# A graph-attention kernel's first-layer node update: bias products on TensorE replaced by adds on VectorE and GpSimd

## The reference, cut to what matters

```python
# layer 0, per node, after the attention sums
out = msgs.reshape(N, H * D) @ Wo + bo
x = out + node_features
mu, var = mean(x), var(x)
layer0 = (x - mu) / sqrt(var + 1e-05) * gamma + beta
x1 = _layernorm(node_features + layer0)
# layer 1, per node
xp = x1 @ W                          # 256 columns; the kernel stores them with the layer's bias less one added
a_src, a_dst = xp . att_src, xp . att_dst   # 4 + 4 columns
```

## Time and profile before

| | us |
|---|---|
| Median of 3 runs | 4633.29 (4626.58 to 4635.58) |
| The profiled execution | 4628.61 |
| Its span, first to last instruction | 4627.2 |
| PE / DVE / ACT / POOL busy in the span | 3929.3 / 3415.2 / 2795.2 / 3143.2 |
| 654 to 2460 us (layer 0's edges at full pace): PE / DVE busy of 1806 | 1710.0 / 1417.4 |

### The profile page before, as it was taken

One profiled execution on the slowest core, in us unless ns is written; L12 is line 12 of the kernel. 1 busy time (PEld: TensorE's weight loads), 2 busy tenths in 40 slices (PEclk: granted clock), 3 DMA queues, 4 the chain that ended last, 5 costly groups with the idle time before them and its releaser, 6 DMA issues. The chain is left out here.

```text
span 4627.2 us, 149696 instructions
## 1 busy us (share of the span) xinstructions
PE 3929.3 (85%) x42462; PEld 2568.6 (56%) x42462; DVE 3415.2 (74%) x11602; ACT 2795.2 (60%) x7985; POOL 3143.2 (68%) x3229
## 2 busy tenths in 40 slices
PE   6988999999999999999996778778877877777874
PEld 4655555555555555555554556555555555555553
DVE  3235788777777778777775578888778778787777
ACT  2324555555555555555553677777777777777775
POOL 1217777777777777777772777777777777777773
PEclk9998999999999999999997677777778777787777
DMA  6878888888888888888884777777777777777774
GB/s 207 282 236 246 259 259 259 257 259 259 259 255 260 258 260 258 257 258 261 259 256 120 187 206 206 207 204 205 207 207 205 205 204 205 205 208 209 203 206 131
DMA packets 820558, 1052.06 MB, mean 227 GB/s; under 512 B 458633, under 2 KB 632338, under 8 KB 820464
## 3 DMA queue, kind: packets, MB, share of 16 engines
q0 software_dynamic: 225072, 726.83, 53.9%
q1 hardware_dynamic: 594078, 323.35, 27.0%
q10 hardware_dynamic: 1314, 0.99, 0.1%
HBM read 915.79 MB, written 133.39 MB: 227 GB/s over the span
## 5 line engine op out<-in xcount | busy, mean ns | idle before, releaser
L1286 POOL DMA_INDIRECT plain_rows<-xp,plain_index x1563 | 1559.8, 998 | 554.9 <-issue 440.8
L765 POOL DMA_INDIRECT typed_rows<-kv,typed_index x1563 | 1511.2, 967 | 626.2 <-issue 414.3
L1391 PE MATMUL plain_p_o<-plain_rows,plain_weight_t 128*64 128x130 f32 (+1 forms) x8336 | 856.5, 348 | 44.0 <-DVE plain_weight_t L1417 43.3
L1158 ACT ACTIVATE typed_weight<-typed_weight,typed_col 128x416 f32<-128x416 f32 x521 | 334.6, 642 | 855.0 <-DVE typed_col L991 809.5
L1378 PE MATMUL plain_p_s<-all_cst,plain_rows 128*128 128x128 f32 (+1 forms) x2084 | 455.0, 318 | 368.2 <-DMA plain_rows<-xp,plain_index 365.9
L1391 PEld LDWEIGHTS plain_p_o<-plain_rows,plain_weight_t 128*64 128x64 f32 (+1 forms) x8336 | 570.2, 169 | 203.8 <-issue 128.5
L1378 PEld LDWEIGHTS plain_p_s<-all_cst,plain_rows 128*128 128x128 f32 (+1 forms) x2084 | 335.2, 174 | 522.6 <-issue 504.8
L989 DVE CUSTOM_DVE_ANT_0 typed_weight<-typed_p_s,typed_far 128x416 f32<-128x416 f32 x521 | 305.1, 586 | 371.5 <-PE typed_p_s L874 347.8
L874 PE MATMUL typed_p_s<-typed_kt,typed_q 64*32 64x416 f32 x4168 | 472.4, 521 | 103.4 <-issue 73.0
L1424 DVE CUSTOM_DVE_ANT_0 plain_alpha<-plain_alpha,plain_far 128x416 f32<-128x416 f32 x521 | 310.0, 595 | 311.4 <-ACT plain_alpha L1540 296.4
L962 DVE TENSOR_TENSOR typed_kt<-typed_p_kt,typed_rel 128x768 f32<-128x768 f32 x521 | 494.7, 950 | 3.7 <-PE typed_p_kt L851 3.4
(11 more groups left out here) (190 smaller groups left out, 6303.5 us busy)
## 6 DMA issues: line engine op xcount, KB each, us to landing
typed_match<-match SPq DMA_DIRECT2D x131, 208.0 KB
plain_match<-match SPq DMA_DIRECT2D x131, 208.0 KB
agg<-qkv_zero SPq DMA_DIRECT2D x98, 264.0 KB
typed_agg<-agg SPq DMA_DIRECT2D x98, 264.0 KB
plain_agg<-agg SPq DMA_DIRECT2D x98, 264.0 KB
kv<-qkv_kv SPq DMA_DIRECT2D x98, 258.0 KB
typed_kinds<-match SPq DMA_DIRECT2D x131, 192.0 KB
typed_rows<-kv,typed_index POOLq DMA_INDIRECT x1563
```

The source lines that it names most:

```text
L765: pool.indirect_dma_start(rows[:, r, j, :], None, k.kv, bass.IndirectOffsetOnAxis(ap=index[:, g, at:at + 1], axis=0)).then_inc(rows_in[r], 16)
L1158: act.activation(weight[:, c], weight[:, c], ACT.Exp, bias=col[:, t.slot(4), LOW:LOW + 1]).then_inc(exp_done, 1)
L1286: pool.indirect_dma_start(rows[:, r, j, :], None, k.xp, bass.IndirectOffsetOnAxis(ap=index[:, g, at:at + 1], axis=0)).then_inc(rows_in[r], 16)
L1391: last = pe.matmul(p_o[at:at + HC, t.slot(2), 0:2 * V], weight_t[0:e, t.slot(2), j * P + at:j * P + at + HC], val[:, 2 * V * g:2 * V * g + ...
```

## The change

Both bias products go. GpSimd's `keep` adds `bo` in place of `beta`, so `p_out` plus `node_rows` is the whole sum of the first norm. VectorE gets a row `shift = beta - bo`, broadcast over 128 partitions, and adds it to `node_rows` between the two instructions of `normalize`, so the second one finds x + beta as before; it waits for the add. ScalarE's `copy_row` keeps the two small copies (the a_src columns and the a_dst columns) and signals `columns_ready`; a new VectorE part `make_row`, `BlockPart(6, 10)`, listed right behind `vary`, waits for that and for the last store of the row, adds `bias_1` while it copies the 256 columns out of `p_1`, and signals `row1_ready`. The set-up loses the three-way splits and three memsets; `bias_1` and the two rows of `shift` come in as rows broadcast to 128 partitions instead of 3. TensorE's wait for `row1_ready` stays where it is.

```diff
 project_nodes, GpSimd
-                pool.tensor_tensor(k.node_rows(t.n), x[:, o], beta[:], ALU.add).then_inc(kept, 1)
+                pool.tensor_tensor(k.node_rows(t.n), x[:, o], bias_o[:], ALU.add).then_inc(kept, 1)
 attend_typed, TensorE, update
-                    pe.matmul(p_out, ones[:], bias_o[:], start=True, stop=False)
                     for a in range(2):
-                        pe.matmul(p_out, message_t[:, a * P:a * P + P], wo[:, a], start=False, stop=a == 1)
+                        pe.matmul(p_out, message_t[:, a * P:a * P + P], wo[:, a], start=a == 0, stop=a == 1)
                 pe.wait_ge(row1_ready, v + 1)
-                pe.matmul(p_1, ones[:], bias_1[:], start=True, stop=False)
                 for a in range(2):
-                    last = pe.matmul(p_1, x1_t[:, a * P:a * P + P], w1[:, a], start=False, stop=a == 1)
+                    last = pe.matmul(p_1, x1_t[:, a * P:a * P + P], w1[:, a], start=a == 0, stop=a == 1)
 VectorE, normalize
                 v.scalar_tensor_tensor(y[:, o], y[:, o], moments[:, 0, o, 0:1], gamma[:], ALU.subtract, ALU.mult).then_inc(centered, 1)
+                v.tensor_tensor(k.node_rows(b.n), k.node_rows(b.n), shift[:], ALU.add).then_inc(shifted, 1)
                 v.wait_ge(centered, b.n + 1)
+                v.wait_ge(shifted, b.n + 1)
 VectorE, new
+            def make_row(b):
+                v.wait_ge(columns_ready, b.n + 1)
+                if not b.known_below(1):
+                    v.wait_ge(row1_out, b.n * 16)
+                v.tensor_tensor(row1[:, 0:VW].rearrange("p (h c) -> p h c", h=HEADS)[:, :, 0:HC], p_1[:, 0:D].rearrange("p (h c) -> p h c", h=HEADS),
+                                bias_1[:].rearrange("p (h c) -> p h c", h=HEADS), ALU.add).then_inc(row1_ready, 1)
 VectorE, set-up: the two splits of seven instructions each are gone
-            for whole, to in ((spare[:, 0], bias_o), (spare[:, 2], bias_1)):
...
 VectorE, order
-                       BlockPart(3, 5, normalize), BlockPart(4, 2, sum_up), BlockPart(4, 8, end_norm), BlockPart(6, 5, vary), BlockPart(5, 0, join),
+                       BlockPart(3, 5, normalize), BlockPart(4, 2, sum_up), BlockPart(4, 8, end_norm), BlockPart(6, 5, vary), BlockPart(6, 10, make_row), BlockPart(5, 0, join),
 ScalarE, copy_row and its loads
-                act.copy(row1[:, VW + P:V1], p_1[:, D + HEADS:W1])
-                act.copy(row1[:, 0:VW].rearrange("p (h c) -> p h c", h=HEADS)[:, :, 0:HC],
-                         p_1[:, 0:D].rearrange("p (h c) -> p h c", h=HEADS)).then_inc(row1_ready, 1)
+                act.copy(row1[:, VW + P:V1], p_1[:, D + HEADS:W1]).then_inc(columns_ready, 1)
-                act.dma_start(spare[:, a], k.i[name].rearrange("(o n) -> o n", o=1).broadcast_to((3, D))).then_inc(weights_in, 16)
+                act.dma_start(to, row(k, name)).then_inc(weights_in, 16)
```

More of the change, by code:

```diff
@@ L529, in project_nodes @@
         q_now = z.sb("q_now", [P, AHEAD, P, 2])
-        beta = z.sb("beta", [P, D])
+        bias_o = z.sb("bias_o", [P, D])
         zero = z.sb("zero", [P, 2, HEADS * AG])
@@ L549, in _ @@
             sp.dma_start(bkv[:, D:2 * D], row(k, "L0_gnn_bv")).then_inc(weights_in, 16)
-            sp.dma_start(beta[:], row(k, "L0_gnn_beta")).then_inc(weights_in, 16)
+            sp.dma_start(bias_o[:], row(k, "L0_gnn_bo")).then_inc(weights_in, 16)
             with nc.allow_non_contiguous_dma(reason="two vectors, once"):
@@ L706, in attend_typed @@
         w1 = z.sb("w1", [P, 2, W1])
-        bias_o = z.sb("bias_o", [P, D], BF16)
-        bias_1 = z.sb("bias_1", [P, W1], BF16)
-        ones = z.sb("ones", [P, P], BF16)
+        shift = z.sb("shift", [P, D])
+        bias_1 = z.sb("bias_1", [P, D])
         gamma = z.sb("gamma", [P, D])
@@ L735, in attend_typed @@
         att = kt[:, 1, 0:2 * D].rearrange("p (s d) -> p s d", s=2)
-        spare = kt[0:3, 1, 2 * D:5 * D].rearrange("p (s d) -> p s d", s=3)
+        old_shift = kt[:, 1, 2 * D:3 * D]
         rel_w = weight[:, 0, 0:3 * P].rearrange("p (s d) -> p s d", s=3)
@@ L744, in attend_typed @@
         (weights_in, agg_in, row1_out, joined, share_ready, message_ready, message_t_ready, turned_both, moved, summed, stats1, moments1,
-         var1, root, inverse, centered, normed, stats2, moments2, var2, x1_ready, x1_t_ready, x1_kept, row1_ready,
+         var1, root, inverse, centered, shifted, columns_ready, normed, stats2, moments2, var2, x1_ready, x1_t_ready, x1_kept, row1_ready,
          settled3, settled4, total_ready) = (z.sem(n) for n in (
             "weights_in", "agg_in", "row1_out", "joined", "share_ready", "message_ready", "message_t_ready", "turned_both", "moved",
-            "summed", "stats1", "moments1", "var1", "root", "inverse", "centered", "normed", "stats2", "moments2", "var2", "x1_ready",
+            "summed", "stats1", "moments1", "var1", "root", "inverse", "centered", "shifted", "columns_ready", "normed", "stats2", "moments2", "var2", "x1_ready",
             "x1_t_ready", "x1_kept", "row1_ready", "settled3", "settled4", "total_ready"))
@@ L1080, in _ @@
             init(v.memset(row1[:], 1.0))
-            for to in (p_w, result, bias_o, bias_1, ones, message, message_t, x1, x1_t):
+            for to in (p_w, result, message, message_t, x1, x1_t):
                 init(v.memset(to[:], 0.0))
@@ L1084, in _ @@
             v.wait_ge(init_done, count)
-            init(v.memset(ones[0:3], 1.0))
             v.wait_ge(weights_in, 16 * WEIGHTS)
             init(v.tensor_scalar(rel_w[:, 0], rel_w[:, 0], 0.2, None, ALU.mult))
-            init(v.tensor_tensor(spare[:, 0], spare[:, 0], spare[:, 1], ALU.subtract))
-            init(v.tensor_scalar(spare[:, 2], spare[:, 2], -1.0, None, ALU.add))
+            init(v.tensor_tensor(shift[:], shift[:], old_shift, ALU.subtract))
+            init(v.tensor_scalar(bias_1[:], bias_1[:], -1.0, None, ALU.add))
             v.wait_ge(init_done, count)
@@ L1195, in _ @@
                 act.dma_start(att[:, a], k.i[name].rearrange("(o h) c -> o (h c)", o=1).broadcast_to((P, D))).then_inc(weights_in, 16)
-            for a, name in enumerate(("L0_gnn_bo", "L0_gnn_beta", "L1_gnn_bias")):
-                act.dma_start(spare[:, a], k.i[name].rearrange("(o n) -> o n", o=1).broadcast_to((3, D))).then_inc(weights_in, 16)
+            for to, name in ((shift[:], "L0_gnn_beta"), (old_shift, "L0_gnn_bo"), (bias_1[:], "L1_gnn_bias")):
+                act.dma_start(to, row(k, name)).then_inc(weights_in, 16)
             act.dma_start(gamma[:], row(k, "L0_gnn_gamma")).then_inc(weights_in, 16)
```

## The result

The changed kernel takes 4964.26 us (median of 4 runs, 4960.27 to 4967.64), the kernel before 4629.93 beside it: ratio 1.0722, 95% interval 1.0703 to 1.074. That is 334 us slower; the prediction said 170 slower, with 4860 as its upper end. The profiled execution has a span of 4966.3 us.

What follows compares the result with a forecast made beforehand. TensorE was taken to set the pace, busy 1710 of 1806 us in layer 0. Row wait 103.6, shift 32, bias products -9, set-up -5.3, tail 4 and clock 47 gave +172 on 4628.6: 4800 us, range 4725 to 4860.

Steps and rivals of the forecast that it cites:

- the row's wait: TensorE's projection waits for VectorE's make_row at tight updates: 56 x 1.85 = +103.6 us, bounds 90 to 118.
- the shift: VectorE's added add inside normalize moves the score 0.33 us later, 98 times: +32 us, bounds 16 to 41.
- the clock: TensorE's new idle lowers its clock at 6 in 10 tight updates: 34 x 1.37 = +47 us, bounds 0 and 77.
- The order of steps 77 and 78: VectorE's step 78 holds make_row behind add_keys, which can't begin before TensorE, ahead of its step 77, reaches the update.
- tight updates: Main-loop updates at steps 16q + 25 and 16q + 13, which need VectorE's steps one later: 56 of 84.
- loose: Updates at steps 16q + 21, needing VectorE's step 82: make_row fits its idle, taken as 0, up to 6 us.
- The tail: After the last tile, ten make_row at 0.41 us: +4 us, up to 12 with new mutual waits.
- The set-up: Removing the splits before the first gather: -5.3 us; the larger row loads taken as nothing, 3 us at worst.
- 1: Rival: the row is late at the projection, but TensorE's clock holds; 4754 us, chance 0.28.
- 2: Rival: the clock falls at nearly every tight update, some spells last twice as long; 4845 us, chance 0.13.
- 3: Rival: TensorE only loses work and the row is ready in time, so faster; 4602 us, chance 0.05.
- 4: Rival: the row is in time, but VectorE's shift costs; 4638 us, about no change, chance 0.06.

Runs made afterwards that it cites:

- after_moved_5: Changed kernel with 120 already-met waits (60 instructions) ahead of VectorE's wait for the weights in the typed set-up; 4820.1 us, ratio 1.041 to the kernel before.
- before_moved: Kernel before with 40 already-met waits (20 instructions) in VectorE's typed set-up; on slower chips 6261.59 us, ratio 1.0196; second run 6322.6 us, 1.0178.
- before_plus6: Kernel before with 12 already-met waits (6 instructions) in VectorE's typed set-up; 4839.45 us, ratio 1.0458.

## Why the prediction was wrong

The step that failed is the sum, 103.6 + 32 - 9 - 5.3 + 4 + 47 = +172: it listed what each engine must do, and had no term for how VectorE's instructions come to it, which is a term put at nothing without a reason. "The plain stage keeps its length" is the sentence in which it shows, since nothing of that stage is changed. Missing were 144 us (4964 less 4820), 137 of them in the typed stage, for VectorE's idles of 4.3 to 6.1 us once per turn. The trace of the kernel before could have warned: no instruction packet between 746 and 2457 us says that no loop is fetched again, and an edit of 14 instructions in VectorE's loop asks whether it still fits. The margin was three to five.

The rest, against after_moved_5, is nearly as worked out: +193 us measured, +172 predicted. No terms cancel by luck: the largest, the row's wait, is close, and the shift and the clock are within their bounds, the clock on the low side.

1. *The order of steps 77 and 78: right.* All 56 tight updates wait for make_row: 50 in the main stretch, 95.9 us, 1.92 each, and six outside it, 10.9 us; together 107 (predicted 56 x 1.85 = 103.6). No loose one does. One of them, which answers to the earlier trace rows:

```profile
1222.02 1.03 PE L901 MATMUL typed_p_t<-typed_wo,typed_message_t 128*128 128x256 f32 x4
...
1224.28 0.15 DVE L1062 TENSOR_SCALAR typed_var<-typed_moments 128x1 f32<-128x1 f32 x1
1224.47 0.42 DVE L1076 TENSOR_TENSOR typed_row<-typed_p_n,typed_bias 128x256 f32<-128x256 f32 x1
1224.95 1.16 PE L904 MATMUL typed_p_n<-typed_w,typed_x_t 128*128 128x264 f32 x4 [1.91 <-DVE typed_row L1076]
```

The idle isn't yet the delay, because the bias products before it are gone. In the kernel before the same update begins with

```profile
1238.59 0.27 PE L901 MATMUL typed_p_t<-typed_bias_o,typed_ones 128*128 128x256 bf16 x1
```

and L907 starts at 1239.68, 1.09 later. Here L904 starts 2.93 behind the update's first product: 1.84 more, and in the median of the 50 it is 1.85. In the loose updates of the main stretch it is 0.87, so there the 0.22 of the bias products is gained.

2. *The shift: right in place and in size.* One normalize, which answers to the earlier trace rows:

```profile
1211.94 0.48 DVE L1047 SCALAR_TENSOR_TENSOR typed_y<-typed_y,typed_moments,typed_gamma 128x256 f32<-128x256 f32 x1
1212.33 0.42 DVE L1048 TENSOR_TENSOR all_x<-all_x,typed_shift 128x256 f32 x1
...
1212.85 0.48 DVE L1051 SCALAR_TENSOR_TENSOR all_x<-typed_y,typed_rstd,all_x 128x256 f32 x1
```

From start to start 0.91 us instead of 0.64, +0.27 (predicted 0.33). The waits before the scores grew by 38 us in the table (predicted 32, within 16 to 41).

3. *The clock: right in kind, on the low side.* TensorE's busy time in the stage rose by 42 us although its bias products, some 98 x 0.22 = 22, are gone: an estimate of 64 for the clock, predicted 47 within 0 to 77. The granted clock of 340 to 2717 is 0.96. In the main stretch it stands at half (1.2 GHz) in 25 spells of 3.41 us, each at one of the 50 tight updates there, where the kernel before has none: half of the updates, where the prediction had 6 in 10.

4. *The tail: on the low side.* The whole stage has 127.5 us of projection waits in 67 places. Without the 56 tight updates 20.8 us are left, all in the tail, against the 11.0 that ScalarE's copy cost there before: 10 more, where I had 4, at most 12.

5. *The set-up: wrong.* The first gather is issued at 349.91 us in the changed kernel and at 350.64 in the earlier trace rows: 0.7 gained, not 5.3. From the stage's first memset on it is 18.2 us instead of 20.3, so 2.1 gained. The splits are gone, but VectorE waits longer for the weights. The kernel before has

```profile
338.85 0.23 DVE L1087 TENSOR_SCALAR typed_weight<-typed_weight 128x128 f32<-128x128 f32 x1 [5.50 <-DMA typed_weight<-in_L_gnn_rel_w]
```

and the changed kernel 9.36 us of idle at the same place; the instruction starts 11.8 us behind the first memset instead of 8.5. That is the term for the loads, which the prediction put at nothing and at 3 us at worst: 3.3. That the loads to 128 partitions instead of 3 make it is the likely cause; no run separates it.

6. *The plain stage: unchanged without the fetching* (2097.0 against 2096.3 us), 10 us longer with it.

Of the rivals, 1 is out since the clock fell, 2 since it fell at half of the tight updates and not at nearly all, with no spell in the main stretch longer than 3.41 us, and 3 and 4 since the row was late.

## What to carry to other kernels

Before you add instructions to a loop, look at the instruction packets on the page and at the length of the compiled loop on each engine: when the packets rise with an edit, look for idle places of one engine, "issue" with no releaser, once per turn. What such an idle costs depends on who stands behind it: 204 us in the typed stage, where TensorE is nearly full and waits for it, and 15 in the plain one, for as many stalls of about the same length. Then try a few instructions of padding ahead of the loop before judging the edit itself; a comparison of two kernels whose loops lie differently measures the place, not the edit. And where work goes from one in-order queue to another, compare steps, not engine totals: the row was late by the order alone, as worked out.

## What the runs showed of the hardware

Six instructions that do nothing, run once in the set-up, make the kernel 4.6% slower; three make no difference. What costs is only where they leave the loop: over three pieces of 128 instructions or over four.

On the slower chips TensorE pauses inside one run of products that wait for nothing that the profile shows. In before_moved (second run) the eight score products, one row of 0.90 us in the earlier trace rows, stand as:

```profile
2012.06 1.16 PE L874 MATMUL typed_p_s<-typed_kt,typed_q 64*32 64x416 f32 x2
2013.48 0.51 PE L874 MATMUL typed_p_s<-typed_kt,typed_q 64*32 64x416 f32 x1 [0.26 <-issue]
2014.51 0.94 PE L874 MATMUL typed_p_s<-typed_kt,typed_q 64*32 64x416 f32 x5 [0.53 <-issue]
```

There the same edit is worth less: the changed kernel 1.0235 instead of 1.0722, and the fetching in one loop costs 1.016 to 1.020 (before_moved) where before_plus6 has 1.0458. The two are placed a little differently; whether that is part of the difference is untried. What makes those chips pause the runs don't show.
